# Score products and maximum pieces on half rows of the array, both heads at a time

## The reference, cut to what matters

```
q = (x @ Wq).reshape(b, n, 8, 64).transpose(0, 2, 1, 3)        # n = 2048
k = (context @ Wk).reshape(b, m, 8, 64).transpose(0, 2, 1, 3)  # m = 1601
v = (context @ Wv).reshape(b, m, 8, 64).transpose(0, 2, 1, 3)
scores = jnp.einsum('bhnd,bhmd->bhnm', q, k) * 64 ** -0.5
attn = jax.nn.softmax(scores, axis=-1)
out = jnp.einsum('bhnm,bhmd->bhnd', attn, v)
return out.transpose(0, 2, 1, 3).reshape(b, n, 512) @ Wo + bo
```

## Time and profile before

| | us |
|---|---|
| median of three runs | 1016.05 |
| the profiled execution | 1015.61 |
| its span, first to last instruction | 1013.8 |
| TensorE busy | 947.1 |
| VectorE busy | 586.0 |
| GpSimd busy | 563.9 |
| ScalarE busy | 360.3 |
| mean granted TensorE clock, share of full | 0.975 |

### The profile page before, as it was taken

The page is one execution under the profiler, slowest core; times in us unless marked ns, Lnnn a source line. Parts: engine busy times, 40 slices in busy tenths (PEclk is TensorE's granted clock), DMA queues, the critical chain, the costliest instruction groups (busy, mean ns, idle before and its releaser), DMA issues. The chain is left out here.

```text
span 1013.8 us, 12662 instructions
## 1 busy us (share of the span) xinstructions
PE 947.1 (93%) x3784; PEld 555.7 (55%) x3785; DVE 586.0 (58%) x1212; ACT 360.3 (36%) x506; POOL 563.9 (56%) x347
## 2 busy tenths in 40 slices
PE   6988699999999999999999999999799999999990
PEld 3544354555565555565554565544478888856650
DVE  6998566677566577666567667564555221134444
ACT  3254244434425434425434434435251211122222
POOL 4452187797776797776797777796103500023335
PEclk9999799999999999999999999999799999999995
DMA  7215600100001100001100001004198100312115
GB/s 266 63 40 145 158 10 11 32 0 11 11 1 38 47 1 12 11 0 48 35 0 11 11 1 53 11 1 146 55 293 291 68 1 0 114 42 84 53 37 166
DMA packets 45730, 60.23 MB, mean 59 GB/s; under 512 B 4072, under 2 KB 35696, under 8 KB 45680
## 3 DMA queue, kind: packets, MB, share of 16 engines
q1 hardware_dynamic: 40160, 53.85, 18.0%
q0 software_dynamic: 2256, 4.21, 1.2%
q10 hardware_dynamic: 3264, 1.57, 0.5%
HBM read 36.45 MB, written 17.59 MB: 53 GB/s over the span
## 5 line engine op out<-in xcount | busy, mean ns | idle before, releaser
L641 POOL TENSOR_TENSOR accG<-accG,probs 128x1024 f32<-128x1024 f32 (+1 forms) x170 | 404.1, 2377 | 60.1 <-ACT probs L675 45.1
L728 DVE TENSOR_REDUCE mxp<-mx 128x1 f32<-128x402 f32 x480 | 260.7, 572 | 97.5 <-PE mx L851 81.3
L675 ACT ACTIVATE probs<-st 128x1024 f32<-128x1024 f32 (+1 forms) x208 | 211.3, 1025 | 279.1 <-PE st L874 155.1
L886 PE MATMUL av<-probs,V 128*64 128x512 f32 (+1 forms) x832 | 192.4, 600 | 0.0
L874 PE MATMUL st<-Q,K 65*128 65x512 f32 (+1 forms) x416 | 159.0, 399 | 0.4 <-DMA Q<-mrow 0.4
L886 PEld LDWEIGHTS av<-probs,V 128*64 128x64 f32 (+1 forms) x832 | 54.1, 136 | 102.4 <-issue 90.2
L851 PE MATMUL mx<-K,Q1b 128*128 128x400 f32 (+1 forms) x256 | 98.3, 384 | 0.9 <-DVE Q1b L716 0.5
L874 PEld LDWEIGHTS st<-Q,K 65*128 65x128 f32 (+1 forms) x416 | 75.6, 185 | 24.7 <-issue 13.0
L851 PE MATMUL mx<-K,Q1a 128*128 128x402 f32 x224 | 85.8, 383 | 0.3
L641 POOL TENSOR_TENSOR accG<-probs 128x1024 f32<-128x1024 f32 x16 | 38.2, 2387 | 80.0 <-ACT probs L675 68.1
L863 PE MATMUL st<-Q1b,K 128*128 128x512 f32 (+1 forms) x208 | 71.5, 426 | 3.4 <-ACT probs L675 3.4
(11 more groups left out here) (197 smaller groups left out, 1181.5 us busy)
## 6 DMA issues: line engine op xcount, KB each, us to landing
w_gate_up<-in_gate_up SPq DMA_DIRECT2D x4, 2048.0 KB, 21.8
w_down<-in_down SPq DMA_DIRECT2D x2, 2048.0 KB, 15.6
xs<-scratch_sorted_x SPq DMA_DIRECT2D x31, 128.5 KB, 2.1
scratch_sorted_x<-zero SPq DMA_DIRECT2D x7, 514.0 KB, 8.3
K<-K SPq DMA_DIRECT2D x8, 400.5 KB, 4.9
xT<-in_xT SPq DMA_DIRECT2D x4, 512.0 KB, 7.9
xring<-in_x SPq DMA_DIRECT2D x4, 512.0 KB, 8.2
scratch_x1b<-xT SPq DMA_DIRECT2D x4, 512.0 KB, 3.1
```

What stands on the lines that cost most here:

```text
L641: pool.tensor_tensor(accG[0:r], so_far[0:r], probs[0:r, (p * KT + t) % RING], ALU.add).then_inc(g_add, 1)
L675: act.activation(probs[0:r, s], st[g % 2][0:r, :], ACT.Exp, scale=DH ** -0.5).then_inc(a_probs, 1)
L728: dve.tensor_reduce(mxp[:, par, u, j:j + 1], mx[(par + n) % 2][:, 0:kn], AX.X, ALU.max).then_inc(v_mx, 1)
L886: mm = pe.matmul(av[h * DH:(h + 1) * DH, :], V[0:r, t, (2 * p + h) * DH:(2 * p + h + 1) * DH], probs[0:r, g % RING, h * QC:(h + 1) * QC], ...
```

## The change

Keys and queries are each kept once, both heads of a pair in the 128 partitions (head h in rows 64h to 64h + 63), as K_hi, K_lo, Q_hi and Q_lo. Every score product and every maximum piece has 64 rows and names one half of the array's rows; the order alternates between the halves, and neighbours write different banks. A tile has eight score products (four parts: high x high, high key x low query, low key x high query, ones x M). M holds the negated maxima in 8 of its 128 rows, made by VectorE from the transpose with a mask. There are 26 pieces, 24 of 512 columns and two of 4 x 66, alternating between the heads and the two banks. The projection stands ahead of all score products of the opening. The copies on SP's queue are gone. Before attention, a key part is one instruction on ScalarE and one on VectorE; the 32 pieces there keep 128 rows, with queries in a buffer that is zero in the other head's rows (Q_alone).

```diff
+def by_head(nm, par):
+    return nm[:, par].rearrange("p (h x) -> p h x", h=2)[:, :, 0:QT]
...
-            def repeat_keys(p):
-
-                sp.wait_ge(a_khi, 2 * len(KC) * (p + 1))
-                for h in (2 * p, 2 * p + 1):
-                    sp.dma_start(K1[DH:P, h, :].bitcast(F32), K1[0:DH, h, :].bitcast(F32)
-                                 ).then_inc(d_dup if p else d_dup0, 16)
...
-            pool.memset(K2[DH:DH + 1, :, :].bitcast(F32), 1.0).then_inc(g_const, 1)
+            pool.memset(nm[:], 0.0).then_inc(g_const, 1)
             pool.wait_ge(g_const, 2)
+            pool.memset(Q_alone[:].bitcast(F32), 0.0).then_inc(g_const, 1)
...
-                for h in range(2):
-                    act.activation(K1[0:DH, 2 * p + h, k0:k0 + kn], banks[4 + n % 2][DH * h:DH * h + DH, 0:kn],
-                                   ACT.Copy).then_inc(a_khi, 1)
+                act.activation(K_hi[:, p, k0:k0 + kn], banks[4 + n % 2][:, 0:kn], ACT.Copy).then_inc(a_khi, 1)
...
-                dve.wait_ge(a_khi, 2 * (n + 1))
-                for h in range(2):
-                    dve.tensor_tensor(K2[0:DH, 2 * p + h, k0:k0 + kn], banks[4 + n % 2][DH * h:DH * h + DH, 0:kn],
-                                      K1[0:DH, 2 * p + h, k0:k0 + kn].bitcast(F32), ALU.subtract).then_inc(v_klo, 1)
+                dve.wait_ge(a_khi, n + 1)
+                dve.tensor_tensor(K_lo[:, p, k0:k0 + kn], banks[4 + n % 2][:, 0:kn], K_hi[:, p, k0:k0 + kn].bitcast(F32),
+                                  ALU.subtract).then_inc(v_klo, 1)
...
-                pe.matmul(banks[2 + (n + 1) % 2][:, 0:kn], Q1[:, h, i * P:(i + 1) * P], K1[:, h, k0:k0 + kn],
+                pe.matmul(banks[2 + (n + 1) % 2][:, 0:kn], Q_alone[:, h, i * P:(i + 1) * P], K_hi[:, 0, k0:k0 + kn],
                           start=True, stop=True).then_inc(p_mx0, 1)
...
-STEP_MX = 1 + 2 * QT * len(KC)
+MC = [(0, 512), (512, 512), (1024, 512), (1536, 66)]
+PIECE_PAIRS = QT * (len(MC) - 1) + 1
+STEP_MX = 1 + 2 * PIECE_PAIRS
...
-PIECES_AT = (1, 1, 3, 3, 3, 3, 3, 3, 2, 3, 3, 2, 2)
-DIVIDE_AFTER = (11, 11, 22, 22)
+MORE_PIECES_AT = 5
+DIVIDE_AFTER = (8, 8, 18, 18)
...
-            def max_row(F, par):
+            def max_rows(F):
                 dve.wait_ge(p_mT, F + 1)
-                dve.tensor_copy(mrow[:, par], misc[0:2 * QT, 0:P]).then_inc(v_mT, 1)
+                dve.tensor_tensor(M[:].rearrange("p (i q) -> p i q", i=QT), misc[:, 0:P].unsqueeze(1).to_broadcast([P, QT, P]),
+                                  mask[:].unsqueeze(2).to_broadcast([P, QT, P]), ALU.mult).then_inc(v_mT, 1)
...
                 pe.wait_ge(v_mx, use + (n - 1))
-                pe.matmul(mx[(par + n) % 2][:, 0:kn], Q1[par][:, h, i * P:(i + 1) * P], K1[:, 2 * pair + h, k0:k0 + kn],
-                          start=True, stop=True).then_inc(p_mx, 1)
+                for a, q in enumerate(range(QT) if i is None else (i,)):
+                    mm = pe.matmul(mx[h][:, a * kn:(a + 1) * kn], Q_hi[par][rows, q * P:(q + 1) * P],
+                                   K_hi[rows, pair, k0:k0 + kn], start=True, stop=True)
+                mm.then_inc(p_mx, 1)
...
+                w, q = ((K_hi[rows, p, keys], Q_hi[p % 2][rows, :]), (K_hi[rows, p, keys], Q_lo[p % 2][rows, :]),
+                        (K_lo[rows, p, keys], Q_hi[p % 2][rows, :]), (ones_r[rows, 0:r], M[rows, :]))[part]
+                mm = pe.matmul(st[g % 2][0:r, h * QC:(h + 1) * QC], w, q, start=(part == 0), stop=(part == MAXIMA))
...
+            def whole_tile(c, p, t, piece):
+
+                free_scores(c, p, t)
+                products(c, p, t, (HIGH, LOW_QUERY))
+                piece()
+                score(c, p, t, LOW_KEY, 1)
+                score(c, p, t, LOW_KEY, 0)
+                score(c, p, t, MAXIMA, 1)
+                score(c, p, t, MAXIMA, 0)
+                piece()
...
-                        q_proj(pair, par)
-                    scores_1(c, p, 1)
+                        q_proj(pair)
+                    for t in range(2):
+                        free_scores(c, p, t)
+                        products(c, p, t, (HIGH, LOW_QUERY, LOW_KEY))
                     if before:
                         values(*before, KT - 1)
                         sums(*before, sum_use(*before))
...
+                        if t == MORE_PIECES_AT:
                             next_piece()
+                            next_piece()
+                        whole_tile(c, p, t, next_piece)
```

More of the change, by code:

```diff
@@ L277, in query_high @@
                 act.wait_ge(p_q0, 1)
+                act.wait_ge(g_const, 3)
+                act.activation(Q_hi[:], banks[2][:], ACT.Copy).then_inc(a_q0, 1)
                 for h in range(2):
-                    act.activation(Q1[0:DH, h], banks[2][DH * h:DH * h + DH, :], ACT.Copy).then_inc(a_q0, 1)
+                    rows = slice(DH * h, DH * h + DH)
+                    act.activation(Q_alone[rows, h], banks[2][rows, :], ACT.Copy).then_inc(a_q0, 1)
             slots(key=key_high, val=value, norm_c=norm_c, tr=transposed, query=query_high)
@@ L352, in query_low @@
             def query_low(_):
[L353 to L356, removed]
+                dve.wait_ge(a_q0, 3)
+                dve.tensor_tensor(Q_lo[:], banks[2][:], Q_hi[:].bitcast(F32), ALU.subtract).then_inc(v_q0, 1)
             def piece_maximum(n):
@@ L543, in parity, with piece_of @@
             return (p + 1) % 2
+        def piece_of(n):
+            k = (n - 1) // 2
+            whole = len(MC) - 1
+            return (None, whole) if k == PIECE_PAIRS - 1 else (k // whole, k % whole)
         block = ctx.enter_context(nc.Block())
@@ L548, in _ @@
         def _(sp):
[L549 to L563, removed]
             def store(c):
@@ L572, in chunk @@
                 for p in range(PAIRS):
[L573 to L576, removed]
                     if p == PAIRS - 2 and not last:
@@ L615, in _ @@
             pool.wait_ge(g_ones, 3)
+            pool.memset(ones_r[:].bitcast(F32), 1.0).then_inc(g_ones, 1)
+            pool.wait_ge(g_ones, 4)
             def inverse(c):
@@ L812, in _ @@
             dve.sem_inc(v_misc, SEED)
-            dve.sem_inc(v_lo, 2)
+            dve.tensor_tensor(mask[:], ident[:, 0:QT], ident[:, DH:DH + QT], ALU.add).then_inc(v_lo, 1)
+            dve.wait_ge(v_lo, 1)
             dve.sem_inc(v_mx, STEP_MX)
@@ L856, in max_transpose, with score @@
                 pe.wait_ge(v_misc, SEED + max_use(c, p))
-                pe.transpose(misc[0:2 * QT, 0:P], nm[:, p % 2], ident[:]).then_inc(p_mT, 1)
-            def scores_1(c, p, t):
+                pe.transpose(misc[:, 0:P], nm[:, p % 2], ident[:]).then_inc(p_mT, 1)
+            def score(c, p, t, part, h):
                 g, r = p * KT + t, rows_of(t)
-                pe.wait_ge(a_probs, c * PAIRS * KT + (g + 1))
-                for h in range(2):
-                    pe.matmul(st[g % 2][0:r, h * QC:(h + 1) * QC], K1[:, 2 * p + h, t * P:t * P + r], Q1[p % 2][:, h],
-                              start=True, stop=False)
@@ L866, in scores_2 @@
-            def scores_2(c, p, t, between=None):
-                g, r = p * KT + t, rows_of(t)
-                par = p % 2
-                if t == 0:
-                    pe.wait_ge(d_q2[par], (c * 2 + (p // 2 + 1)) * 16)
-                    pe.wait_ge(d_m[par], (c * 2 + (p // 2 + 1)) * 32)
[L873 to L877, removed]
-                mm.then_inc(p_qk, 1)
+                rows, keys = slice(DH * h, DH * h + DH), slice(t * P, t * P + r)
@@ new lines, in score, with products @@
+                w, q = ((K_hi[rows, p, keys], Q_hi[p % 2][rows, :]), (K_hi[rows, p, keys], Q_lo[p % 2][rows, :]),
+                        (K_lo[rows, p, keys], Q_hi[p % 2][rows, :]), (ones_r[rows, 0:r], M[rows, :]))[part]
+                mm = pe.matmul(st[g % 2][0:r, h * QC:(h + 1) * QC], w, q, start=(part == 0), stop=(part == MAXIMA))
+                if part == MAXIMA:
+                    mm.then_inc(p_qk, 1)
+            def products(c, p, t, parts):
+                for part in parts:
+                    for h in range(2):
+                        score(c, p, t, part, h)
@@ L1718, in program @@
                                     ("mxp", [P, 2, TILE_U, len(KC)], F32),
-                                    ("nm", [P, 2, TILE_U], F32)):
+                                    ("nm", [P, 2, P], F32)):
                 mem[name] = ctx.enter_context(nc.sbuf_tensor(name, shape, dt))
-            mem["Q1"] = [ctx.enter_context(nc.sbuf_tensor("Q1a", [P, 2, QC], F32R))]
+            mem["Q_hi"], mem["Q_lo"] = ([ctx.enter_context(nc.sbuf_tensor(f"{part}{i}", [P, QC], F32R)) for i in range(2)]
+                                        for part in ("Q_hi", "Q_lo"))
             before_attention(nc, io, mem)
```

116 lines of the change are left out of this document (57 added, 59 removed).

## The result

The changed kernel takes 979.48 us (median of 4 runs, 976.84 to 979.89), the kernel before 1017.04 on the same chip: a ratio of 0.962, 95% interval 0.960 to 0.965. The forecast was 966 us, its range 954 to 995. The sign held, the overlap of the two row halves held, and the time lies in the range, 13.5 us above the forecast. What was to set the step next, GpSimd alone, did not come out so.

The account below looks back on a forecast made before the run. TensorE was taken to set the pace, with GpSimd next. Plain steps -31.5, output steps -9.6, first interval -4.2, last step +0.9 and before attention -5.0 gave -49.4 from 1015.6: 966 us, range 954 to 995.

Parts of the forecast that it names:

- Halves side by side, slot 0.235: Score products and pieces: a pair on the two row halves costs about one product, 0.235 us.
- B: Rival, half-row products: each load stands in the open, slot 0.335 us, step 39.1, total 1059 us; chance 0.09.
- C: Rival, half-row products: the halves don't run together at all, slot 0.46 us, total 1189 us; chance 0.05.
- D: Rival, half-row products: slot of 0.29 us, the parts cancel, 1013 to 1019 us; chance 0.03.
- TensorE's own step, 32.6: Plain attention step: TensorE's opening, tiles, extra pieces and value bursts sum to 32.6 us, 3.5 less than 36.08.
- Tile 1.28: Tiles of a plain step: five slots 1.18 us plus 0.10 for a load in the open, 1.28 us each.
- rival A: Tiles: VectorE sets the pace, 0.70 us a reduction, 1.50 a tile, step 35.0, total 994 us; chance 0.23.
- GpSimd is late next: Plain steps: GpSimd's adds 29.2 us plus 3.7 allow no step under 32.9; forecast 33.2, 31.5 us saved over 11.
- Output step 3.2 less: The three steps with the output projection inside: no matter of GpSimd, 3.2 us less each, 9.6 in all.
- First interval -4.2: First attention step interval: 2.9 us less, and 1.3 less for its opening.
- Before attention -5.0: Key parts before attention: half of the low-part instructions go, 5.0 us less, between 3.4 and 6.8.
- Last step +0.9: Last attention step: GpSimd is later in it by what TensorE gained; 0.9 us lost.

Follow-up runs that it names:

- the run on one half: Changed kernel with all score products and maximum pieces of both heads reading rows 0 to 63, head 1's part left out: 1177.31 us.
- both helpers relieved: Changed kernel with 11 GpSimd additions a step over 512 of 1024 columns and VectorE's 512-column reductions over 256: 961.18 us, ratio 0.945.
- GpSimd relieved: Changed kernel with 11 of GpSimd's 12 additions a step over 512 of 1024 columns: 973.54 us, ratio 0.957.
- that reorder: Changed kernel with maxima products and tile 0's and 1's exponentials ahead of last values and sums, ScalarE's values copy behind these exponentials: 963.22 us, ratio 0.948.
- four-and-four: Changed kernel listing head 0's four products of a tile, then head 1's four, one piece ahead and one behind: 1019.13 us.
- two-and-two: Changed kernel, pieces in place, the four products between pieces listed two of one head, then two of the other: 978.36 us, ratio 0.963.

## Why the prediction was right, and by what it was off
- **Halves side by side, slot 0.235**: right, 0.23 measured, and shown by the run on one half. Rivals B, C and D fall. "TensorE: Matmul & The Clock Gate", Part 3, of the Trainium skill has a weight load overlap a running product only where the row groups differ (its text on the mechanism also lets in a load into the background weight buffer). Of two products on the same rows the run on one half has the next start 0.23 us later (431.18 to 431.64 for two), loads included: the measurement decides against the rule that only differing row groups overlap, as the earlier trace rows had it.
- **TensorE's own step, 32.6**: right in the first and last chunk (32.57 with both helpers relieved), 0.6 too low in the middle ones. The middle two chunks are the body of a loop; whether that is the cause no run took apart.
- **Tile 1.28**: 1.35 in tiles 2 to 4 (4.04 / 3), 1.30 in 9 to 12 without the 0.38 priced for the last two pieces, but (6.25 - 0.34) / 4 = 1.48 in 5 to 8 without the 0.34 priced for the two more pieces there. With both helpers relieved the first chunk's tiles 5 to 8 take 5.60 us, (5.60 - 0.34) / 4 = 1.31: the price was TensorE's, and the excess is VectorE's, rival A in one group of three. Ten reductions at 0.655 need 6.55 us; I had priced VectorE by two pieces a tile and had not added up the group with ten.
- **"GpSimd is late next", no step under 32.9, forecast 33.2**: this is the step that failed, by 0.6 us in each of 11 steps, 6.8 us. GpSimd's own limit in the first chunk is 33.7: its first idle time is 4.11 and not 3.7 us, and its second stays (0.46 here, 1.14 in the earlier trace rows), since its fifth add doesn't start ahead of the exponential of tile 5, whose products stand behind the first burst. I let that gap vanish: 29.2 + 4.11 + 0.46 = 33.8. VectorE has a limit of its own, 33.5 to 33.9. So neither engine alone holds the step.
- **Output step 3.2 less**: 2.0, 3.7 us short in three. With both helpers relieved they are 40.4, 40.4 and 39.8 us, 2.8 less than before on the mean: two thirds of what was missing are the helpers' here too. The prediction had put them at nothing in this step.
- **First interval -4.2**: as measured, but in part by luck: it counts 2.9 for the step, the gain forecast for a plain one, and plain steps gained 2.25; no run separates its other part.
- **Before attention -5.0**: 7.2, with about 6.6 from the halved instructions. Counting nothing for the eight key instructions ahead of 59.3 us, or half for those behind 89, was too little; which, no run tells.
- **Last step +0.9**: +3.2 from the last transpose to the end, of which 1.8 lie in the step, up to the end of its sums (37.6 us, 35.8 before). The last chunk's adds stand back to back and the sums wait for them:
```profile
617.22 27.54 POOL L625 TENSOR_TENSOR accG<-accG,probs 128x1024 f32<-128x1024 f32 x11
```
```profile
640.16 0.33 PE L846 MATMUL misc<-ident,nm 128*128 128x128 f32 x1
...
644.82 1.08 PE L900 MATMUL misc<-accG,ones 128*64 128x512 f32 x4 [1.73 <-POOL accG L625]
```
  The sums stand 4.66 us behind the transpose (2.69 before, 682.21 to 684.90), 2.0 us more; with GpSimd relieved the step is 1.9 us shorter (35.7). The other 1.4 us lie behind attention (297.2 us from there to the end, 295.8 before), in stages that the change leaves alone: in 40 us there the granted clock was 0.83 (680.16 to 720.16), 0.87 before (722.21 to 762.21). They are not the forecast's.
- **Sum**: 6.8 + 3.7 + 2.3 - 2.2 = 10.6 us of the 10.9 between 966 and the profiled 976.84 (the last 2.3 are 0.9 in the last step and 1.4 behind attention); the median lies 2.6 us above that execution.

## What to carry to other kernels
Where a change speeds up the engine in front, add up each helper's work between two points where it must be done, not over the whole step or per tile: here ten reductions in one group and an add that waits behind a burst took 0.65 and 0.46 us that no busy share showed. Two helpers with limits close together hide each other, so relieving one tells little by itself; relieve each and then both. Nor does the busy share of the engine in front clear its helpers: it was busy 32.59 us of a step in which a helper held it up, and 31.83 for the same products without. Work for another engine's latency (exponentials, first pieces) belongs ahead of work that nobody waits for (last values, sums): that reorder gave 16 us more without changing a single product.

## What the runs showed of the hardware
- Products on rows 0 to 63 and on rows 64 to 127 ran together also where the list had up to three of the same half between them: four-and-four took 0.94 us for eight, and two-and-two the same time as in turn (978.36 and 979.48 us). The second half's products started ahead of earlier listed ones of the first half.
- A product of 64 rows takes as long as one of 128: 0.23 us for 512 columns alone on its half. Only pairing gains.
- A reduction of 512 columns took 0.64 to 0.655 us in a row of ten; a 1024-column add on GpSimd 2.39 us alone and 27.54 / 11 = 2.50 in a row.
- With both helpers relieved a plain step takes 32.57 us in the chunk written out and 33.21 inside the loop, where TensorE is busy 31.83 and 32.03 of it: two thirds of the difference are idle time. The cause is open.
- TensorE's granted clock was 0.50 in the 5 us in which its wait of 2.65 us for GpSimd ended; the changed kernel kept 1.00 through the same step.
